# A graph layer on one core: h0's fp16 halves of six of eight tile pairs are transposed by DMA, and the wide product runs one pair later

## The reference

```
h   = relu(layernorm(x))
g   = h @ W_sa
s_l = g @ a_sa[0, :256];  s_r = g @ a_sa[0, 256:]
e   = where(adj != 0, exp(-leaky_relu(s_l[:, None] + s_r[None, :], 0.01)), 0)
x_a = (e / (e.sum(1) + 1e-5)) @ g
x_b = adj @ (h @ W_gcnb) + b_gcnb
attn_a = sigmoid([adj @ h, h] @ Wa.T + ba);  attn_b = sigmoid([adj @ h, h] @ Wb.T + bb)
out = x + sigmoid(attn_a * x_a + attn_b * x_b)
```

## Time and profile before

| | |
|---|---|
| median of three runs | 182.56 us |
| profiled execution, its own time | 182.3 us |
| its span | 180.5 us |
| TensorE busy in the span | 175.3 us, 97% |
| VectorE busy | 146.5 us, 81% |
| ScalarE busy | 115.8 us, 64% |
| DMA, mean over the span | 88 GB/s |
| granted TensorE clock | 1.00 in every slice |

### The profile page before, as it was taken

How to read it: one execution, slowest core, us unless ns; L and a number is a source line. 1 busy time by engine, 2 the same in 40 slices (tenths; PEclk the granted TensorE clock), 3 DMA queues, 4 the chain that set the end, 5 groups by cost and what they waited for, 6 DMA issues and landing times.

```text
span 180.5 us, 3416 instructions
## 1 busy us (share of the span) xinstructions
PE 175.3 (97%) x1335; PEld 128.7 (71%) x1335; DVE 146.5 (81%) x306; ACT 115.8 (64%) x170; POOL 17.8 (10%) x39
## 2 busy tenths in 40 slices
PE   7899999999999999999999999999999999999993
PEld 2656776664544448888864468888888888888892
DVE  1759989748899999599999920999999999987542
ACT  3358788963999987748395640494785686673410
POOL 2544364230000200000000000000000000000000
PEclk9999999999999999999999999999999999999999
DMA  5998967899980598000001100000010010011101
GB/s 172 303 298 143 189 102 162 154 220 241 244 310 5 87 205 172 0 4 0 2 4 58 58 0 4 0 0 0 4 58 0 4 60 0 4 60 56 64 29 29
DMA packets 4767, 15.81 MB, mean 88 GB/s; under 512 B 528, under 2 KB 1040, under 8 KB 3856
## 3 DMA queue, kind: packets, MB, share of 16 engines
q0 software_dynamic: 1440, 8.39, 24.3%
q1 hardware_dynamic: 3312, 7.22, 11.3%
HBM read 21.90 MB, written 2.10 MB: 133 GB/s over the span
## 4 chain that ended last, share of the span: by engine, by line
PE 91%; DMA 7%; DVE 0%; issue 0%; ACT 0%; DVEq 0%
PE ps L730 31%; PE ps L754 16%; PE ps L755 16%; PE ps L753 16%; PE ps L746 6%; PE ps L704 5%; DMA adj<-in_adj_t 5%; DMA x_sb<-in_x 2%; PE ps L693 2%; PE ps L715 1%; DVE logit L673 0%; ACT logit L370 0%; DVE res L589 0%; DVEq L672 0%
## 5 line engine op out<-in xcount | busy, mean ns | idle before, releaser
L753 PE MATMUL ps<-mv_lo,e_hi 128*128 128x257 f16 (+2 forms) x272 | 71.0, 267 | 0.0
L755 PE MATMUL ps<-mv_hi,e_lo 128*128 128x257 f16 (+2 forms) x272 | 70.9, 266 | 0.0
L754 PE MATMUL ps<-mv_hi,e_hi 128*128 128x257 f16 (+2 forms) x272 | 70.8, 266 | 0.0
L336 ACT ACTIVATE z<-z,log_e 128x1024 f32<-128x1024 f32 x32 | 36.7, 1147 | 29.0 <-DVE z L526 29.0
L730 PE MATMUL ps<-adj,nat_hi 128*128 128x512 f16 x128 | 48.5, 379 | 0.2 <-DMA adj<-in_adj_t 0.2
L730 PE MATMUL ps<-adj,nat_lo 128*128 128x512 f16 x128 | 48.5, 379 | 0.0
L526 DVE SCALAR_TENSOR_TENSOR z<-sl_row,exs,far 128x512 f32<-128x512 f32 x64 | 45.1, 746 | 0.0
L534 DVE TENSOR_TENSOR e_lo<-z,e_hi 128x1024 f16<-128x1024 f32 x32 | 39.0, 1219 | 1.3 <-ACT e_hi L346 1.3
L346 ACT ACTIVATE e_hi<-z 128x1024 f16<-128x1024 f32 x32 | 33.3, 1041 | 0.0
L754 PEld LDWEIGHTS ps<-mv_hi,e_hi 128*128 128x128 f16 x272 | 26.5, 98 | 3.2
L753 PEld LDWEIGHTS ps<-mv_lo,e_hi 128*128 128x128 f16 x272 | 26.4, 97 | 3.3
(11 more groups left out here) (69 smaller groups left out, 184.8 us busy)
## 6 DMA issues: line engine op xcount, KB each, us to landing
adj<-in_adj_t POOLq DMA_DIRECT2D x7, 1024.0 KB, 9.7
x_sb<-in_x SPq DMA_DIRECT2D x7, 512.0 KB, 11.4
out<-res SPq DMA_DIRECT2D x7, 256.0 KB, 2.0
x_sb<-in_x SPq DMA_DIRECT2D x2, 256.0 KB, 4.1
adj<-in_adj_t POOLq DMA_DIRECT2D x2, 256.0 KB, 7.1
adj<-in_adj_t POOLq DMA_DIRECT2D x1, 512.0 KB, 5.7
c_sb<-in_consts SPq DMA_DIRECT2D x1, 258.0 KB, 3.5
wa_sb<-in_w_wide SPq DMA_DIRECT2D x1, 258.0 KB, 3.7
```

The source lines that it names most:

```text
L336: act.activation(z[:, n % ZRING, :, :], z[:, n % ZRING, :, :], ACT.Exp, bias=log_e[:, 0:1], scale=SLOPE - 1.0).then_inc(exp_done, 1)
L753: pe.matmul(ps[:, bank, cols], e_hi[:, s, i1], mv_lo[:, j, cols], start=(j == 0), stop=False)
L754: pe.matmul(ps[:, bank, cols], e_hi[:, s, i1], mv_hi[:, j, cols], start=False, stop=False)
L755: return pe.matmul(ps[:, bank, cols], e_lo[:, s, i1], mv_hi[:, j, cols], start=False, stop=(j == NT - 1))
```

## The change

`turn`, `h0t_highs` and `h0t_lows` stay for pairs 0 and 1 alone. For pairs 2 to 7 SyncE issues two transposing DMAs, from `nat_hi` to `h0t_hi` and from `nat_lo` to `h0t_lo`, each 128 partitions x 4 blocks of 128 fp16 (128 KB), as soon as the half is there. `wide(u)` waits for both. The layout of `h0t` changes from (k, node) to (tile, k, node). `wide(u - 1)` now stands behind the `b_products` of pair u; for the last pair it stands between the two tiles. The PSUM banks of even and odd pairs are exchanged, and ADJ pieces 6 and 7 are issued only after the transposes of pair 5.

```diff
-WIDE_BANKS = (2, 6)
+NTURN = 2
+WIDE_BANKS = (6, 2)
...
-            sp.wait_ge(turned, NU)
+            for u in range(NTURN, NU):
+                ts = slice(2 * u, 2 * u + 2)
+                for have, nat, h0t in ((nat_high, nat_hi, h0t_hi), (nat_ready, nat_lo, h0t_lo)):
+                    sp.wait_ge(have, u + 1)
+                    sp.dma_start(h0t[:, ts, :, :].rearrange("p t k n -> p (t k) n"),
+                                 nat[:, ts, :].rearrange("p t d -> p (t d)"),
+                                 transpose=True).then_inc(h0t_landed[u - NTURN], 16)
+            sp.wait_ge(turned, NTURN)
...
+            pool.wait_ge(h0t_landed[5 - NTURN], 32)
             load_adj(6)
...
@@ ScalarE @@
-            for u in range(NU):
-                if u + 1 < NU:
-                    h0t_highs(u + 1)
-                if u + 2 < NU:
-                    h0_tiles(u + 2)
-                if u + 1 < NU:
-                    nat_highs(u + 1)
-                mv_highs(u)
+            h0t_highs(1)
+            h0_tiles(2)
+            nat_highs(1)
+            mv_highs(0)
+            for u in range(2, NU):
+                nat_highs(u)
+                if u + 1 < NU:
+                    h0_tiles(u + 1)
+                mv_highs(u - 1)
+            mv_highs(NU - 1)
...
@@ VectorE, from u = 2 @@
+                nat_lows(u)
+                if u + 2 < NU:
+                    moments(u + 2)
+                narrow_results(u - 1)
+                mv_lows(u - 1)
...
             def wide(u):
-                pe.wait_ge(h0t_ready, u + 1)
+                if u < NTURN:
+                    pe.wait_ge(h0t_ready, u + 1)
+                else:
+                    pe.wait_ge(h0t_landed[u - NTURN], 32)
...
@@ b_products @@
-                    pe.wait_ge(mv_ready, NT)
+                    pe.wait_ge(mv_ready, NT - 2)
...
-            for u in range(1, NU):
-                if u + 1 < NU:
-                    turn(u + 1)
-                wide(u)
-                b_products(0, 2 * u, 2 * u + 2)
+            wide(1)
+            b_products(0, 2, 4)
+            b_products(0, 4, 6)
+            for u in range(3, NU):
+                b_products(0, 2 * u, 2 * u + 1)
+                if u == NU - 1:
+                    wide(u - 1)
+                b_products(0, 2 * u + 1, 2 * u + 2)
+                if u < NU - 1:
+                    wide(u - 1)
+            wide(NU - 1)
```

More of the change, by code:

```diff
@@ L115, in build @@
         e_lo = sb("e_lo", [P, 2 * ESLOT, CW], F16)
-        h0t_hi = e_hi[:, 16:24, :].rearrange("p (k s) n -> p k (s n)", k=KT)
-        h0t_lo = e_lo[:, 16:24, :].rearrange("p (k s) n -> p k (s n)", k=KT)
+        h0t_hi = e_hi[:, 16:24, :].rearrange("p s (a k n) -> p (s a) k n", k=KT, n=P)
+        h0t_lo = e_lo[:, 16:24, :].rearrange("p s (a k n) -> p (s a) k n", k=KT, n=P)
         zeros = e_hi[:, 0, :]
@@ L164, in build @@
         h0t_ready = sem("h0t_ready")
+        h0t_landed = [sem(f"h0t_landed{u}") for u in range(NTURN, NU)]
         wide_product = sem("wide_product")
@@ L208, in turn_bank @@
         def turn_bank(u):
-            return ps[:, u % 2, :].rearrange("p (k n) -> p k n", k=KT)
+            return ps[:, u % 2, :].rearrange("p (t k n) -> p t k n", t=2, k=KT)
         block = ctx.enter_context(nc.Block())
@@ L309, in h0t_highs @@
                 act.wait_ge(turned, u + 1)
-                act.activation(h0t_hi[:, :, 2 * u * P:(2 * u + 2) * P], turn_bank(u),
+                act.activation(h0t_hi[:, 2 * u:2 * u + 2, :, :], turn_bank(u),
                                ACT.Copy).then_inc(h0t_high, 1)
@@ L481, in h0t_lows @@
                 dve.wait_ge(h0t_high, u + 1)
-                cols = slice(2 * u * P, (2 * u + 2) * P)
-                dve.tensor_tensor(h0t_lo[:, :, cols], turn_bank(u), h0t_hi[:, :, cols],
+                ts = slice(2 * u, 2 * u + 2)
+                dve.tensor_tensor(h0t_lo[:, ts, :, :], turn_bank(u), h0t_hi[:, ts, :, :],
                                   ALU.subtract).then_inc(h0t_ready, 1)
@@ L601, in _ @@
             moments(2)
-            for u in range(NU):
-                if u + 1 < NU:
[L604 to L607, removed]
-                if u + 1 < NU:
-                    nat_lows(u + 1)
-                mv_lows(u)
+            h0t_lows(1)
+            moments(3)
+            narrow_results(0)
+            nat_lows(1)
+            mv_lows(0)
+            for u in range(2, NU):
+                nat_lows(u)
[3 more added lines that the diff above has]
+                mv_lows(u - 1)
+            narrow_results(NU - 1)
+            mv_lows(NU - 1)
             w_post_low()
@@ L687, in turn @@
             def turn(u):
-                if u >= 2:
-                    pe.wait_ge(h0t_ready, u - 1)
                 for t in range(2 * u, 2 * u + 2):
@@ L692, in turn @@
                     for k in range(KT):
-                        ins = pe.transpose(turn_bank(u)[:, k, t % 2 * P:(t % 2 + 1) * P], x_sb[:, t, k * P:(k + 1) * P], ident[:, :])
+                        ins = pe.transpose(turn_bank(u)[:, t % 2, k, :], x_sb[:, t, k * P:(k + 1) * P], ident[:, :])
                 ins.then_inc(turned, 1)
             def wide(u):
-                pe.wait_ge(h0t_ready, u + 1)
+                if u < NTURN:
+                    pe.wait_ge(h0t_ready, u + 1)
+                else:
+                    pe.wait_ge(h0t_landed[u - NTURN], 32)
                 if u == 0:
@@ L703, in wide @@
                     for i, (k, a, b) in enumerate(three):
-                        ins = pe.matmul(ps[:, WIDE_BANKS[u % 2] + t % 2, 0:WA], h0t[a][:, k, t * P:(t + 1) * P],
+                        ins = pe.matmul(ps[:, WIDE_BANKS[u % 2] + t % 2, 0:WA], h0t[a][:, t, k, :],
                                         wa2[b][:, k, :], start=(i == 0), stop=(i == len(three) - 1))
@@ L710, in sl_rows @@
                 if c < 2:
-                    pe.wait_ge(h0t_ready, NU)
+                    pe.wait_ge(h0t_ready, NTURN)
                 else:
```

## The result

| | before | after |
|---|---|---|
| median of the runs | 182.73 us (182.02 to 183.7, 4 runs) | 210.92 us (209.65 to 212.19, 4 runs) |
| ratio | | 1.154, 95% interval 1.147 to 1.161 |
| span of the profiled execution | 180.5 us | 209.5 us |
| start of `sl_rows(0)`, the end of the first stage | 38.80 us | 67.82 us |

Some executions of a kernel take over 1.5% longer than its fastest; they are listed with the others, and the ratios leave them out.

A forecast was written before the change was run, and what follows sets the result against it. TensorE, busy 97% of the span, was taken as the bound. The profiled 182.3 us, less 2.8 for transposes, plus 13.4 of stalls and 1.1 for landing, gave 194.0, median 194.2; own range 191 to 198, with rivals 191 to 208.

The forecast's parts named there:

- Off TensorE: First stage: six transpose steps leave TensorE, saving 2.8 us.
- The way round: First stage, wide product through scale and halves to the next adjacency products: TensorE idles 2.86 us, four times.
- The first stall: TensorE waits 1.9 us before the adjacency products of pair 3, for that pair's low half.
- Behind the stage: Check of later weights, adjacency pieces 6 and 7 and x reloads: each adds 0.
- The landing: Transposing DMAs in the first stage land in 4.1 us; only pair 7 is late, by 1.1 us.
- upper bound of 9.2: Slowest landing row, 129 KB behind other loads in 9.2 us; at that, transposes add 11.6 us over the stalls.
- The clock: Rival, chance 0.08: idle TensorE falls to 1.2 GHz, 15 us more over five pairs, 209 us; half of that, 202.
- late landings: Rival, chance 0.20: transposes alternating with adjacency packets land near 9.2 us, adding 11.6 us, 205 us in all.

The follow-up runs named there:

- halves ahead: The changed kernel with ScalarE and VectorE writing each pair's halves one step earlier; 201.8 and 204.5 us, ratio 1.112 to the kernel before.
- loop alone: The changed kernel without transposing DMAs or landing waits, later wide products reading halves of pairs 0 and 1; 196.3 and 197.9 us, 1.079 to the kernel before.
- halves ahead, no transposes: The changed kernel with halves written one step earlier and no transposing DMAs or landing waits; 185.2 and 185.5 us, ratio 1.014 to the kernel before.

## Why the prediction was wrong

The direction and the mechanism named for it were right, the size was not: 194.2 us (191 to 208) against 210.9.

- **Off TensorE, 2.8 us.** Six times four products are gone, and the sum of terms above, 29.0 us, comes out with it. No run shows it as a gain, since in each something else is late.
- **The way round, 2.86 us per period.** Right: 2.79 us of idle time, 2.95 counted as the forecast did, four times, before the pairs named. With landings out and the clock held it was 193.9 for 193.3 us.
- **The first stall, 1.9 us before pair 3.** Right, but in the profiled execution a wait stands in its place that I had not looked for: adjacency piece 2 could be used 1.8 us earlier than before (at 18.08 for 19.84 us) and came at 19.9. The part "Behind the stage" checked pieces 6 and 7, not this one. Where piece 2 comes in time, the predicted stall is there: 1.77 us with the transposes not waited for, 1.78 with the clock held.
- **The landing, taken at 4.1 us.** This step failed: its term in the sum was 1.1 us, and it measured 13.5. A transpose landed in 2.3 to 3.2 us where the adjacency loads left the DMA engines free, and in 8 to 14 us beside them (one in 5.2), over the upper bound of 9.2. What was wrong was the kind of row: I took the 4.1 us of a load that met little traffic, though the text itself says that both queues are busy together until 50 us. Which pairs were late was wrong too. I had pair 7 alone; TensorE waited 3.45 us for pair 2 and 6.16 us for pair 6, and not for pair 7. The stalls did not bring this about. The program issues pieces 6 and 7 as soon as pair 5 has landed, ahead of pair 6's transposes: its low half took 13.0 us with no landing waited for, and 15.9 with the halves ahead. The 13.5 us are the changed kernel less the same kernel without landing waits, 197.4 us, with the clock behind the waits in them.
- **The clock, a rival at 0.08 and nothing in the sum.** It fell. 7.7 us of stretched work are in the trace. Holding it gave 3.2 us in the loop alone and 2.2 us in the profiled execution of the changed kernel, where it could not be held to the end. The earlier trace rows lie around a gap of 0.69 us; they could not tell about 2.8. The Trainium skill, "TensorE: Matmul & The Clock Gate", "Part 1: The HAM clock gate", says that an idle array falls back to 1.2 GHz, and here the trace agrees: PEclk 0.50 behind waits of 2.8 us and more, though not behind each of them.
- **The steps from one run to the next.** 182.7 before; 193.9 with the way round alone (forecast 193.3); 197.1 with its clock; 197.4 with the twelve DMAs issued; 210.9 with their landings waited for. This is one order of adding the costs. In another they have other sizes, as the 17.7 us above show.
- **The chances.** The rivals were treated as cases of which one comes, at 205 and 209 us, and the range ended at 208. All three costs came together: the way round and the late landings each stand without the other, and either kind of wait lowered the clock. 10.6 for the way round and 11.6 for late landings leave 6 us of the 28, less than the 15 put on the clock; the forecast had no sum of this kind.

## What to carry to other kernels

When one engine's work is moved later against the others, draw the ring of who waits for whom again and count the work that lies between its two ends; a distance in pairs on one engine means nothing if another engine's order has changed. Price a small DMA by what is on the DMA engines at its hour, not by its size: here the small packets issued beside 3 MB of large ones landed with the large ones. And don't treat rivals that can come together as cases of which one comes: here every kind of wait also lowered the clock.

## What the runs showed of the hardware

- A transpose of 128 x 512 fp16 from SBUF to SBUF took SyncE 1.2 to 1.3 us to issue on a quiet queue, and up to 4.5 us beside 3 MB of loads (at 52.88 us; 9.5 us in the run with the halves ahead). It landed in 2.3 to 2.7 us on quiet engines, and in the changed kernel in 8 to 14 us beside the loads, one in 5.2. An estimate of its share is 0.8 us of the 16 engines' time.
- Both sides of the sharing pay, but not alike. Two 1 MB loads took 1.1 and 2.5 us longer with transposes beside them (8.9 for 7.8 us, 10.2 for 7.7); a transpose beside 3 MB of loads took over five times its quiet 2.4 us (13.5).
- Gaps of the same 2.8 us left the granted clock at 1.00 once and at 0.50 three times in one execution, both in the changed kernel and in the loop alone. Gaps of 1.5 us left it at 1.00 (halves ahead, no transposes).
